# Slots 0 to 5 of an expert layer: one 128-row copy out of PSUM, and an accumulating DMA into the slots' table

## The reference, cut to what matters

```python
t = x.reshape(-1, d)                      # 384 tokens, d = 1024
logits = t @ switch_w + switch_b
route_prob_max = jnp.max(jax.nn.softmax(logits, axis=-1), axis=-1)
routes = jnp.argmax(route_prob, axis=-1)
for e in range(8):
    h = jax.nn.gelu(t @ w1[e] + b1[e])    # w1[e]: 1024 x 512
    y = h @ w2[e] + b2[e]                 # w2[e]: 512 x 1024
    out = jnp.where((routes == e)[:, None], y, out)
out = out * route_prob_max[:, None]
```

## Time and profile before

| | |
|---|---|
| Median of 3 runs | 640.7 us (638.69, 640.7, 641.32) |
| Profiled execution | 638.88 us, of which its span from first to last instruction is 637.1 us |
| PE (TensorE matmul) busy | 566.1 us, 89% of the span |
| DVE busy | 456.7 us, 72% |
| ACT busy | 317.7 us, 50% |
| POOL busy | 177.4 us, 28% |
| Hardware DMA queue q1 (SP's) | 90.02 MB, 41.6% of 16 engines |
| Software DMA queue q0 (POOL's) | 11.72 MB, 6.7% |
| Mean granted TensorE clock | 0.967 of full |

### The profile page before, as it was taken

The page is one execution under the profiler, slowest core; times in us unless marked ns, Lnnn a source line. Parts: engine busy times, 40 slices in busy tenths (PEclk is TensorE's granted clock), DMA queues, the critical chain, the costliest instruction groups (busy, mean ns, idle before and its releaser), DMA issues.

```text
span 637.1 us, 9209 instructions
## 1 busy us (share of the span) xinstructions
PE 566.1 (89%) x3090; PEld 517.5 (81%) x3090; DVE 456.7 (72%) x806; ACT 317.7 (50%) x474; POOL 177.4 (28%) x168
## 2 busy tenths in 40 slices
PE   2799999999999999999999999999898679888860
PEld 2699997888999999999898888899786567766650
DVE  6688887876454444735679889787889465999952
ACT  3445553320333333443466764675662336998940
POOL 5566765765399000710001022100001100000001
PEclk9889999999999999999999999999999969999985
DMA  8365558450533444485232343422563203999926
GB/s 301 131 198 176 171 163 243 114 127 1 201 129 111 158 133 132 128 255 150 78 99 67 99 99 100 105 99 83 215 199 105 81 19 123 347 412 412 411 58 214
DMA packets 32963, 102.69 MB, mean 161 GB/s; under 512 B 5376, under 2 KB 9536, under 8 KB 32928
## 3 DMA queue, kind: packets, MB, share of 16 engines
q1 hardware_dynamic: 27792, 90.02, 41.6%
q0 software_dynamic: 4992, 11.72, 6.7%
q10 hardware_dynamic: 144, 0.52, 0.3%
HBM read 96.65 MB, written 5.60 MB: 160 GB/s over the span
## 4 chain that ended last, share of the span: by engine, by line
PE 54%; DVE 24%; ACT 7%; issue 6%; DMA 6%; POOL 1%; DVEq 0%; ACTq 0%; POOLq 0%; SPq 0%
PE ps L1482 31%; DVE wsp L901 7%; PE ps L1496 5%; DVE big L901 4%; DMA raw<-in_w_experts 3%; PE ps L1661 2%; ACT work L713 2%; PE ps L1615 2%; PE ps L1590 2%; PE ps L1552 2%; PE ps L1533 2%; PE ps L1751 2%; ACT wsp L592 2%; DVE pt L901 2%; PE ps L1605 1%
## 5 line engine op out<-in xcount | busy, mean ns | idle before, releaser
L1482 PE MATMUL ps<-big,wsp 128*128 128x384 f32 x1680 | 304.3, 340 | 9.0 <-DVE wsp L901 5.8
L1482 PEld LDWEIGHTS ps<-big,wsp 128*128 128x128 f32 x1680 | 294.8, 190 | 13.5 <-DVE wsp L901 5.6
L901 DVE TENSOR_TENSOR wsp<-raw,wsp 128x1024 fp32r<-128x1024 f32 x117 | 150.2, 1295 | 29.6 <-ACT wsp L592 23.9
L592 ACT ACTIVATE wsp<-raw 128x1024 fp32r<-128x1024 f32 x83 | 87.2, 1053 | 33.3 <-PE ps L1496 12.9
L464 POOL TENSOR_SCALAR rs<-mv 128x1 f32<-128x1 f32 x12 | 10.4, 868 | 198.3 <-DVE mv L1221 100.7
L508 POOL DMA_INDIRECT edge_table<-ef,eidx x48 | 55.8, 1163 | 32.6 <-DMA edge_table<-ef,eidx 18.5
L599 ACT ACTIVATE big<-ps,bias 128x384 f32 x24 | 14.0, 583 | 81.0 <-PE ps L1482 81.0
L912 DVE SCALAR_TENSOR_TENSOR big<-ps,bias,big 128x384 f32 x24 | 14.8, 618 | 51.5 <-ACT big L599 51.5
L901 DVE TENSOR_TENSOR big<-raw_x,big 128x1024 fp32r<-128x1024 f32 x36 | 42.0, 1216 | 0.3 <-ACT big L764 0.3
L764 ACT ACTIVATE wsp<-raw 128x1024 fp32r<-128x1024 f32 x34 | 34.5, 1048 | 6.7 <-DMA raw<-in_w_experts 4.1
L1803 PE MATMUL ps<-wsp,big 128*128 128x512 f32 x112 | 28.7, 398 | 9.2 <-DVE big L901 9.2
(11 more groups left out here) (243 smaller groups left out, 840.1 us busy)
## 6 DMA issues: line engine op xcount, KB each, us to landing
raw<-in_w_stream SPq DMA_DIRECT2D x85, 512.0 KB, 3.4
raw<-in_w_experts SPq DMA_DIRECT2D x32, 512.0 KB, 6.5
raw_x<-in_w_experts SPq DMA_DIRECT2D x32, 512.0 KB, 6.5
rowbuf<-in_rowb POOLq DMA_DIRECT2D x6, 512.0 KB, 6.7
raw_x<-in_w_stream SPq DMA_DIRECT2D x4, 512.0 KB, 7.0
slot_y<-maskb POOLq DMA_DIRECT2D x8, 256.0 KB, 5.6
tok<-in_x SPq DMA_DIRECT2D x3, 512.0 KB, 4.1
edges_a<-in_src_rows SPq DMA_DIRECT2D x8, 192.0 KB, 4.1
```

Of the source, the lines that this page charges most:

```text
L592: nc.scalar.activation(wsp[:, 0, slot, :], raw[:, slot, :], ACT.Copy).then_inc(w_hi, 1)
L901: return nc.vector.tensor_tensor(dst, value, hi.bitcast(F32), ALU.subtract)
L1482: ins = nc.tensor.matmul(ps[:, bank, 0:N], wsp[:, a, slot, k * P:(k + 1) * P], moving[:, b, k, :], start=(k == 0 and n == 0), stop=(k == K ...
```

## The change

For slots 0 to 5 (`PLAIN = 6`), ACT copies all 128 rows of the product out of PSUM in one instruction, in turn into two buffers (`maskb` and `row_buf`). DVE does nothing for these slots. POOL writes the upper 64 rows of the copy into the table with a plain DMA, waits until it has landed, and issues a second DMA of the lower 64 rows that adds to what the table holds. ACT may overwrite a copy buffer when the second DMA of the slot two before has landed (`y_added`). TensorE may reuse the PSUM banks of a slot once its copy is done (`y_copied`) rather than its sum (`y_sum`). Slots 6 and 7 go as before, and since they use the same buffers, ACT's copy of slot 6 waits for the second DMAs of all six slots. At the end POOL reads the count of extra slots once, ahead of the waits for the DMAs.

```diff
+PLAIN = EXPERTS - 2
+        y_both = [maskflat[:, 0:D], row_buf[:]]
         y_buf, y_tmp = maskflat[0:SLOT, 0:D], row_buf[0:SLOT, :]
...
-            for s in range(EXPERTS):
-                pool.wait_ge(y_sum, s + 1)
+            for s in range(PLAIN):
+                rows = ys_dram[s * SLOT:(s + 1) * SLOT, :]
+                pool.wait_ge(y_copied, s + 1)
+                pool.dma_start(rows, y_both[s % 2][0:SLOT, :]).then_inc(y_stored, 16)
+                pool.wait_ge(y_stored, 16 * (s + 1))
+                pool.dma_start(rows, y_both[s % 2][SLOT:P, :], accum_op=ALU.add).then_inc(y_added, 16)
+            for s in range(PLAIN, EXPERTS):
+                pool.wait_ge(y_sum, s - PLAIN + 1)
                 pool.dma_start(ys_dram[s * SLOT:(s + 1) * SLOT, :], y_buf).then_inc(y_out, 16)
+            pool.wait_ge(pos_done, 1)
             over = pool.value_load(rowi[0:1, OVER:OVER + 1], min_val=0, max_val=OVER)
             with pool.If(over > 0):
...
-            pool.wait_ge(pos_done, 1)
-
-            pool.wait_ge(y_out, 16 * EXPERTS)
-            over = pool.value_load(rowi[0:1, OVER:OVER + 1], min_val=0, max_val=OVER)
-            with pool.If(over > 0):
-                pool.wait_ge(y_out, 16 * SLOTS)
+            pool.wait_ge(y_added, 16 * PLAIN)
+            pool.wait_ge(y_out, 16 * (EXPERTS - PLAIN))
...
+            def both_halves_of_y(e):
+
+                act.wait_ge(y_ready, ys.add())
+                if e >= 2:
+                    act.wait_ge(y_added, 16 * (e - 1))
+                nc.scalar.activation(y_both[e % 2], whole(4 + 2 * (e % 2)), ACT.Copy).then_inc(y_copied, 1)
+
             def low_rows_of_y(e):
 
                 act.wait_ge(y_ready, ys.add())
-                if ys.n > 1:
-                    act.wait_ge(y_sum, ys.n - 1)
+                act.wait_ge(y_added, 16 * PLAIN)
+                if ys.n > PLAIN + 1:
+                    act.wait_ge(y_sum, ys.n - PLAIN - 1)
...
-                low_rows_of_y(e)
+                if e < PLAIN:
+                    both_halves_of_y(e)
+                else:
+                    low_rows_of_y(e)
...
-                rows_of_y(e)
+                if e >= PLAIN:
+                    rows_of_y(e)
...
-                if y_no.n > 1:
-                    pe.wait_ge(y_sum, y_no.n - 1)
+                if 1 < y_no.n <= PLAIN + 1:
+                    pe.wait_ge(y_copied, y_no.n - 1)
+                if y_no.n > PLAIN + 1:
+                    pe.wait_ge(y_sum, y_no.n - PLAIN - 1)
```

More of the change, by code:

```diff
@@ L281, in graph_layer @@
         y_ready, y_low, y_sum, y_out = sem("y_ready"), sem("y_low"), sem("y_sum"), sem("y_out")
+        y_copied, y_stored, y_added = sem("y_copied"), sem("y_stored"), sem("y_added")
         yg_in = [sem(f"yg_in{t}") for t in range(NT)]
@@ L564, in _ @@
                 for s in range(EXPERTS, SLOTS):
-                    pool.wait_ge(y_sum, s + 1)
+                    pool.wait_ge(y_sum, s - PLAIN + 1)
                     pool.dma_start(ys_dram[s * SLOT:(s + 1) * SLOT, :], y_buf).then_inc(y_out, 16)
-            pool.wait_ge(pos_done, 1)
-            pool.wait_ge(y_out, 16 * EXPERTS)
-            over = pool.value_load(rowi[0:1, OVER:OVER + 1], min_val=0, max_val=OVER)
-            with pool.If(over > 0):
-                pool.wait_ge(y_out, 16 * SLOTS)
+                pool.wait_ge(y_out, 16 * (SLOTS - PLAIN))
+            pool.wait_ge(y_added, 16 * PLAIN)
+            pool.wait_ge(y_out, 16 * (EXPERTS - PLAIN))
             for t in range(NT):
@@ L1398, in rows_of_y @@
                     dve.wait_ge(y_out, 16 * (ys.n - 1))
+                else:
+                    dve.wait_ge(y_added, 16 * PLAIN)
                 nc.vector.tensor_tensor(y_buf, whole(4 + 2 * (e % 2))[0:SLOT, :], y_tmp, ALU.add).then_inc(y_sum, 1)
```

## The result

The changed kernel takes 651.45 us in the median of 4 runs (648.51 to 652.96), against 640.46 us (638.69 to 641.32) for the kernel before in the same comparison. The ratio is 1.0162 with a 95% interval of 1.0134 to 1.019: it is 1.6% slower, 8.6 to 12.2 us. The forecast was 648.8 us, slower, with a range of 642.5 to 654.5.

The account below looks back on a forecast made before the run. The prediction took a full DMA pipe to bound the kernel, DVE within a few per cent. Terms -0.4 + 5.1 + 4.1 + 0.5 - 1.2 = 8.1 us on 640.7 gave 648.8 us, range 642.5 to 654.5.

Parts of the forecast that it names:

- What bounds the kernel: In the expert stream, a full DMA pipe (share 1.02 to 1.03, 411 GB/s) sets 10.8 us per expert, DVE close behind.
- The faster rival: In the stream, buffers released at DVE's pace limit the DMA, so DVE's relief comes through: -4.3 us, 636.4; chance 0.05.
- The sixth sum: After the stream, DVE no longer sums slot 5 and takes up gelu(6) sooner: -0.4 us.
- The 128-row copy: On ACT, copying 128 rows instead of 64 takes no longer, about 1.02 us: no change.
- The second DMA in the stream: In the full pipe, accumulates of slots 0 to 3 delay block 58, 1.27 us each: +5.1 us (2.6 to 6.4).
- the plain price of the range: Low end for one accumulate in the stream: what its bytes cost as a plain write, 0.64 us.
- The price from the SBUF accumulates: High end for one accumulate in the stream: half the 3.2 us of 512 KB accumulates into SBUF, 1.6 us.
- The wait at slot 6: ACT's copy of slot 6 waits for slot 5's second DMA, need 9.8 us against room 5.7: +4.1 us.
- The clock in down(7): After a longer idle stretch TensorE starts down(7) at its 1.2 GHz level: +0.5 us (0 to 1.3).
- POOL's tail: At the end, reading the count and branching no longer stand behind the last landing: -1.2 us (-0.65 to -1.3).
- the two large terms: The accumulates' toll in the stream, +5.1 us, and the stall of ACT's copy of slot 6, +4.1 us.
- One of the signs that I named: In the profile after, through the stage, the DMA's bytes per us stay at about 411 GB/s.

Follow-up runs that it names:

- e2: The changed kernel without the second DMA, so the lower halves are left out of the result: ratio 0.9999 to the kernel before, 10.82 us per expert.
- e5: The kernel before, DVE's sums included, plus an accumulating DMA into an unread spare table for each of slots 0 to 5: ratio 1.0138.
- e6: The kernel before without the table writes of slots 0 to 5, DVE still summing them: ratio 0.9983, 10.55 us per expert.
- e7: The changed kernel without either DMA of slots 0 to 5, whose results are left out: ratio 0.9919 to the kernel before, 10.2 us per expert.
- e3: The changed kernel with slots 6 and 7 summed in place in the two copy buffers, so slot 6 waits only for second DMAs of slots 0 to 4: ratio 1.0051.
- e1: The changed kernel with its second DMA as a plain write that adds nothing: ratio 1.0083 to the kernel before, 11.4 us per expert.
- e4: The kernel before with only the changed end of POOL's program, the count read once ahead of the waits for table writes: ratio 0.9967.
- e10: The same kernel as e4, run once more beside the kernel before on the same chip: ratio 0.997.

## Why the prediction was right

**What bounds the kernel.** Right, and it carried the rest. The step from a DMA share of 1.02 and DVE's idle time to "DVE's relief is worth nothing" was borne out to 0.01 us per expert by e2 (10.82), and e5 shows the same pace with the sums kept. The share by itself would not have borne it: e6, which DVE paces, has 1.02 as well, because the two bounds lie within 3% of each other. The first experts are a case of this. Before, their sums are 10.55 us apart, DVE's own pace, up to slot 2; still e2 needs no less from slot 0 to slot 5 (55.28 against 54.87). The faster rival was wrong in its mechanism, and e7 gives the size of what it was after: 0.3 us per expert, if the table writes were not there at all.

**The sixth sum, -0.4.** It fits: 0.5 in e3 and e7.

**The 128-row copy, nothing.** Right: 1.00 to 1.01 us.

**The second DMA in the stream, +5.1.** Right mechanism, somewhat too large. The term was four times c = 1.27, taken as twice a plain write's price. Measured are 1.1 per accumulate, both in the changed kernel (4.4 for four) and in e5 (5.5 for five). e1 splits it by the period: 0.6 for the bytes, which is the plain price of the range, and 0.5 for the addition. By engine time an accumulate does cost twice a plain write (80 against 40 us per MB, 1.3 us of all engines). Why only 1.1 of it shows in the pace is open in part: from slot 3 to slot 5 the share is 1.034 where it was 1.027, and the weights cost 39.5 us per MB and not 39.9, each worth some 0.1 us per expert. The price from the SBUF accumulates, 1.6, was too high. The Trainium skill's rule on two disjoint halves (DMA: Bandwidth & Descriptors, Rules for kernel authors) holds for e1, where the second half costs what its bytes cost; for an accumulate it gives only half of the toll. By that rule the sum would have been 5.6 against 8.1; the prediction says 5.5 and 8.0, a slip.

**The wait at slot 6, +4.1.** Right mechanism, too small. The room was as worked out: 5.6 us from the end of slot 5's copy (611.41) to slot 6's earliest start (617.0). The need was 11.4 instead of 9.8: 0.28, then 6.83 for the plain write where I took the median 5.6 of the kernel before, 0.29 where I took 0.1, and 3.94 where I took 3.8. So the mis-sized term is the plain write's landing. It is 6.8 to 7.1 us for slot 5 in the three kernels with a second DMA per slot (e1 and e3 too), 5.5 in e2 and 4.5 before, which have no second DMA. Why is open. Other plain writes of the changed kernel took 5.6 to 6.9 us, slot 0's, with none of POOL's ahead of it, 6.8; slot 4's second DMA, which landed 6.5 us after 605.76, was in flight for only 0.6 us of slot 5's write; and in e2 and before, single writes of other slots took up to 7.1 and 6.9 us. e3 measures the stall itself: 5.8 us.

**The clock in down(7), +0.5.** The two profiles give 0.8. TensorE was idle for 7.64 us ahead of it, and down(7) took 6.8 us against 6.0:

```profile
625.49 3.78 PE L1826 MATMUL ps<-big 128*128 128x512 f32 x8 [7.64 <-DVE big L919]
...
631.91 0.39 PE L1832 MATMUL ps<-big,qp 128*128 128x512 f32 x1
```

But in e1, after 6.81 us of idle time, it took 5.8, and the one program of e4 and e10 took 4.4 and 6.0 us for it in its two profiles, after 1.85 us of idle time in both. So one pair of profiles can't show that the longer wait cost 0.8, and this term stays unproven.

**POOL's tail, -1.2.** Measured -1.0 by the stretch, but only 0.75 of it where the term puts it, between landing and gather; 0.3 more lies behind the gathers. I had said that the gather would follow the landing within 0.5 us; it follows by 0.84. What the term left out is that the changed kernel waits for two semaphores ahead of the gather. With one, in e4 and e10, the gather does follow by 0.3 us and the gain is 1.3, so most of the 0.88 us of unexplained issue time can go; with two, 0.79 of it stays.

**The sum.** +9.5 in the stage against +8.1, the two large terms erring to opposite sides. The medians differ by 11.0, with an interval of 8.6 to 12.2, and nothing that I read explains the part beyond 9.5. The profiled execution was forecast at 647.0 and took 652.61; of these 5.6 us, 4.3 lie ahead of the stage. That the median came within 2.7 us of the forecast is in part luck: 0.7 too much in the stream, 1.7 too little in the stall. One of the signs that I named was wrong: bytes per us fell to 395 and did not stay at 411, because an accumulate holds the engines for twice as long as its counted bytes say. The share, 1.03, stayed as I had said. ACT's waits for the weights are 4.5 us in the three whole experts, 1.5 each, as expected.

## What to carry to other kernels

Before work is moved from an engine to a DMA, read the DMA engines' share in that stretch. In this stream, at 1.02 to 1.03, every byte that was added came out of the stream that the engines wait for. The share alone does not name the bound (e6 had 1.02 with DVE setting the pace); a kernel with the engine's work taken out, as e2, does. And the relief of the engine is worth only its distance to the next bound, here 0.0 us with the table writes in the stream and 0.3 without them, for 1.1 us of work per expert. An accumulating DMA costs twice its bytes' engine time, and as it must wait for the write below it, two landings lie in a row (11.4 us here); whoever reuses its source buffer near the end of a stage, when nothing else covers it, waits for both. Where a buffer that was freed earlier can be used for the last steps, as in e3, such a stall goes: 5.8 us here, at no cost that the profile shows. And at the end of a chain, the kernels that wait for one semaphore were 0.5 us quicker than those that wait for two.

## What the runs showed of the hardware that I had not expected

- An accumulate of 256 KB from SBUF into the table in device memory takes twice the engine time of a plain write of the same bytes (80 against 40 us per MB), but slows a full stream by 1.1 us and not 1.3. Its issue on POOL takes 0.84 us against 0.54. Behind the weight stream (slot 5's second DMA) it lands after 3.9 us, and the plain write in its place after 2.9 (e1), but see the next point.
- One and the same plain write of 256 KB, slot 7's, behind the weight stream, lands after 2.8 to 4.0 us in the twelve profiles. What decides it is open.
- The first gather follows the last landing by 0.3 us where POOL waits for one semaphore and by 0.84 where it waits for two, in nine of nine profiles.
- TensorE's clock in down(7) differs from run to run of one and the same program by 1.6 us: e4 and e10 are the same kernel, and their down(7) had the full clock in the one and, for part of it, the 1.2 GHz level in the other (7.07 and 8.69 us from slot 6's copy to slot 7's).
